# Twenty-two halves of the shared expert units moved beside the first group's score maxima

## What is computed

```python
xn = layernorm(x)                                    # x: (4, 1024, 256)
q, k, v = xn @ Wq + bq, xn @ Wk + bk, xn @ Wv + bv   # 16 heads of 16
attn = softmax(where(causal, q @ k.T / sqrt(16), -inf)) @ v
scores = softmax(xn @ gate_w.T)                      # (4096, 16)
w, idx = top_k(scores, 4);  w = w / sum(w)
routed = sum_e combine[:, e] * ((silu(xn @ w_gate[e]) * (xn @ w_up[e])) @ w_down[e])
shared = (silu(xn @ sw_gate) * (xn @ sw_up)) @ sw_down
out = x + (attn @ Wo + bo) + routed + shared
```

## Time and profile before

| | us |
|---|---|
| median of 3 runs | 1351.32 (1346.31 to 1351.62) |
| the profiled execution, in all | 1356.54 |
| its span, first to last instruction | 1354.9 |
| PE busy in the span | 1007.9 |
| DVE busy | 866.0 |
| ACT busy | 654.5 |
| POOL busy | 579.2 |
| mean granted TensorE clock | 0.88 of full |

### The profile page before, as it was taken

The page is one execution under the profiler, slowest core; times in us unless marked ns, Lnnn a source line. Parts: engine busy times, 40 slices in busy tenths (PEclk is TensorE's granted clock), DMA queues, the critical chain, the costliest instruction groups (busy, mean ns, idle before and its releaser), DMA issues.

```text
span 1354.9 us, 26394 instructions
## 1 busy us (share of the span) xinstructions
PE 1007.9 (74%) x8634; PEld 525.7 (39%) x8634; DVE 866.0 (64%) x1784; ACT 654.5 (48%) x1219; POOL 579.2 (43%) x531
## 2 busy tenths in 40 slices
PE   2788121010399999898998989998988989899885
PEld 1555010000144444444544444454444445444433
DVE  6888831000288887777777676676767676677553
ACT  3778100000154545565566666556666665566341
POOL 6333177776200000454366666435656553464100
PEclk9888555555599999899999999999989999899888
DMA  6899450010113131443545355354535353444702
GB/s 175 270 297 283 125 180 1 1 34 1 43 56 105 54 104 48 88 85 75 89 80 112 63 111 95 66 89 78 111 57 112 56 112 64 88 71 73 134 17 31
DMA packets 99484, 126.41 MB, mean 93 GB/s; under 512 B 24873, under 2 KB 83514, under 8 KB 98834
## 3 DMA queue, kind: packets, MB, share of 16 engines
q0 software_dynamic: 41632, 60.79, 25.0%
q1 hardware_dynamic: 57730, 63.99, 16.1%
HBM read 71.63 MB, written 57.80 MB: 96 GB/s over the span
## 4 chain that ended last, share of the span: by engine, by line
PE 53%; DVE 10%; another core or an unknown queue 10%; issue 9%; ACT 2%; SPq 1%; DMA 1%; POOL 0%; ACTq 0%; DVEq 0%
PE gup L1221 12%; PE pvp L1144 10%; PE outs L1248 9%; DVE part L1314 6%; PE smp L1100 6%; PE turn L1233 4%; PE stp L1125 4%; PE outs L1151 3%; PE turn L1191 3%; PE smp L1083 1%; ACT probs L1484 1%; DVE hf L1371 1%; DVE sg L1366 1%; DMA Qs<-nm 1%
## 5 line engine op out<-in xcount | busy, mean ns | idle before, releaser
L1484 ACT ACTIVATE probs<-stp 128x1024 f32<-128x1024 f32 (+1 forms) x320 | 300.4, 939 | 424.4 <-remote 205.2
L1314 DVE TENSOR_REDUCE part<-smp 128x2 f32<-128x256 f32 (+2 forms) x372 | 345.9, 951 | 140.0 <-remote 72.5
L942 POOL DMA_INDIRECT XG<-xrow_d,slots x144 | 146.8, 1019 | 247.0 <-DMA out<-Y 201.7
L1221 PE MATMUL gup<-gu_w,XC 128*128 (+1 forms) x1152 | 212.8, 321 | 32.7 <-issue 21.8
L1100 PE MATMUL smp<-Ks,Qs 48*128 48x128 f16 (+2 forms) x744 | 112.5, 341 | 103.7 <-DVE part L1314 52.4
L1248 PE MATMUL outs<-dn_w,h 88*128 (+1 forms) x1248 | 183.6, 280 | 0.1
L949 POOL DMA_INDIRECT out<-Y,slots x72 | 117.1, 1626 | 139.1 <-ACT Y L1517 107.8
L1144 PE MATMUL pvp<-probs,Vs 128*32 128x512 f32 (+3 forms) x1536 | 168.8, 512 | 0.8 <-DVE probs L1413 0.7
L949 POOL DMA_INDIRECT acc_d<-Y,slots x72 | 114.7, 1594 | 123.7 <-ACT Y L1517 104.6
L1221 PEld LDWEIGHTS gup<-gu_w,XC 128*128 128x128 f16 x1152 | 107.2, 99 | 96.1 <-issue 43.5
L931 POOL DMA_INDIRECT slot_d<-entry,slot_i x128 | 124.3, 971 | 41.6 <-issue 41.6
(11 more groups left out here) (170 smaller groups left out, 1109.6 us busy)
## 6 DMA issues: line engine op xcount, KB each, us to landing
rb<-rsum_d SPq DMA_DIRECT2D x60, 128.0 KB
Ks<-k_d SPq DMA_DIRECT2D x96, 64.0 KB
Qs<-q_d SPq DMA_DIRECT2D x96, 64.0 KB
v_d<-V SPq DMA_DIRECT2D x8, 544.0 KB, 4.6
Vs<-v_d SPq DMA_DIRECT2D x16, 272.0 KB, 3.0
acc_d<-YA SPq DMA_DIRECT2D x1, 4224.0 KB
X<-L_attn_x POOLq DMA_DIRECT2D x8, 512.0 KB, 5.0
xrow_d<-XR SPq DMA_DIRECT2D x8, 512.0 KB, 5.0
```

What stands on the lines that cost most here:

```text
L942: pool.indirect_dma_start(XG[:, q].rearrange("p a c t -> p (a c t)"), None, s.xrow_d, bass.IndirectOffsetOnAxis(ap=slots[:, r, 0:1], axis= ...
L1221: last = pe.matmul(gup[:, 0:2 * I], columns[:, a, h], weights_of(s.gu_w, e, b, h, slice(0, 2 * I)), start=n == 0, stop=n == 5)
L1314: last = dve.tensor_reduce(part[:, g % 2, k0 // CH, :, j, t], banks[:, :, col:col + w], AX.X, ALU.max)
L1484: act.activation(to, of, ACT.Exp, scale=float(DK) ** -0.5 / QS ** 2).then_inc(exp_done, 1)
```

## The change

The planner takes `PRE = 22` halves off the list first and puts them into steps (-1, 0) to (-1, 21), one each; they are firsts of the units 0 to 11 and seconds of 0 to 9. The rest is spread over the slots as before, with a smaller cost per slot; and while the slot is below `READY = 50` the first half of unit 47, the last one before the routed rows, is held back. On PE, DVE and ACT the head becomes a loop of 22 steps: in each of the first 18 a piece of the maxima and then the half of the step, in the last four only the half; `turn_max(0)` comes in step 19 ahead of the half, `close_max(0)` and `send_to_rows(0)` on DVE in step 18. On SP the columns and rows of tiles 0 and 1 come first, then the loads and stores that belong to the halves of steps 0 to 17, then `send_max(0)`, then the two clears, then what belongs to steps 18 to 21.

```diff
+            for m in range(PRE):
+                (first, second)[halves[i][0]][-1, m] = halves[i][1]
+                i += 1
+            per_slot = (sum(cost[i:]) + sum(fixed_work(g, n) for g, n in every)) / (len(every) - SPARE)
             for k, x in enumerate(every):
                 used += fixed_work(*x)
                 for _ in range(2):
+                    if k < READY and i < len(halves) and halves[i] == (0, SU - 1):
+                        continue
...
-        LAG, SPARE = 2, 4
+        LAG, SPARE, PRE, READY = 2, 4, MP + 4, 50
...  (SP)
+            for t in range(2):
+                shared_columns(t)
+                shared_rows(t)
+            for m in range(MP):
+                after_halves(-1, m)
+            send_max(0)
             sp.wait_ge(a_const, 2)
             sp.dma_start(s.acc_d.rearrange("(t p) d -> p t d", p=P),
                          YA[:, 0:1].broadcast_to([P, TT + 1, D])).then_inc(cleared, 16)
             sp.dma_start(s.out[ST * P:T, :], s.xf[ST * P:T, :]).then_inc(cleared, 16)
-            for t in range(2):
-                shared_columns(t)
-                shared_rows(t)
-            send_max(0)
+            for m in range(MP, PRE):
+                after_halves(-1, m)
...  (PE)
-            for m in range(MP):
-                max_piece(0, m, (smp, stp)[m % 2], m - 1)
-            turn_max(0)
-            pe.wait_ge(red_done, MP)
+            for m in range(PRE):
+                if m < MP:
+                    max_piece(0, m, (smp, stp)[m % 2], m - 1)
+                if m == MP + 1:
+                    turn_max(0)
+                if (-1, m) in FIRST:
+                    gate_up(FIRST[-1, m])
+                else:
+                    z = SECOND[-1, m]
+                    turn_h(z)
+                    if z:
+                        down(z - 1, projected)
+                    youts = outs_before(z)
+            pe.wait_ge(red_done, MP)
...  (DVE)
-            for m in range(MP):
-                reduce_piece(0, m, (smp, stp)[m % 2])
-            close_max(0)
-            send_to_rows(0)
+            for m in range(PRE):
+                if m < MP:
+                    reduce_piece(0, m, (smp, stp)[m % 2])
+                if m == MP:
+                    close_max(0)
+                    send_to_rows(0)
+                if (-1, m) in FIRST:
+                    silu_times_up(FIRST[-1, m])
+                else:
+                    low_part(SECOND[-1, m])
+                    after_second(SECOND[-1, m])
...  (ACT)
+            for m in range(PRE):
+                if (-1, m) in FIRST:
+                    gates(FIRST[-1, m])
+                else:
+                    second_half(SECOND[-1, m])
```

## The result

The changed kernel takes 1391.96 us (median of six runs, 1388.21 to 1395.03), the kernel before 1351.47 beside it: 1.0297 times as long, 95% interval 1.0267 to 1.0328. The forecast was 1366, slower by 1.1%. So the sign was right and the size was not: +40 us of median, +36.7 of span, where +15 had been worked out.

A forecast was written before the change was run, and what follows sets the result against it. PE was taken to set the pace outside a stall of late results from POOL's dense indirect DMAs. 26 + 2.5 - 21 + 1.5 + 5 + 1 = +15 us: span 1370, median 1366; range 1318 to 1392 (own 1359 to 1375).

The forecast's parts named there:

- the stall, its cause and its end: POOL's dense indirect DMAs make PE's results late, 2.8 us a matmul; the stall ends at 362 as before.
- Count by 362: Matmuls PE gets through until 362, halves and maxima together: about 125, against 159 in the kernel before.
- two unknowns: In the count by 362: 20 more matmuls, or 12 fewer if scatters take effect some 4 us earlier; neither taken.
- The 13 steps: Head steps of maxima pieces and halves left after 362: 26 us taken, ends 19.5 and 39.
- slots 0 and 1: Their score pieces, done by 362 in the kernel before, now come on top: 2.5 us.
- the row of maxima: From the send of the first maxima to the first score matmul, overlapping steps 20 and 21: +1.5 us.
- The clears: PE waits near slot 2 for columns queued behind the moved clears: +5 us, ends 0 and 12.
- The light slots: Slots 45 to 49 hold no half and are bound by score, exponential and hops: +1 us, ends 0 and 5.
- The halves out of the slots: 20 halves leave the good stage, their PE work nearly all time: -21 us, ends -13 and -23.
- The fourth rival: Poor overlap in the head, steps over 2.8 us, and clears at full cost: +35 us, 1386; chance 0.16.

The follow-up runs named there:

- with 32 rows: Kernel before with the 128 scatters of slot entries carrying 32 rows in place of 128, nothing between them (result incomplete): 1352.61 us, one run.
- both edits: Changed kernel with the two clears sent right after the first four loads and the first routed half not held to slot 50: 1367.46 us, ratio 1.0104.
- The thin kernel: Kernel before with two matmuls in place of six in the gate and up product of 40 routed halves (80 to 119): 1350.30 us, ratio 0.9973.

## Why the prediction was right or wrong

**Right: the stall, its cause and its end.** The stall is in its place with the same 2.8 us a matmul, the halves share it with the maxima and don't fill it, and the scatters make it (156 us, and the graded runs with spaced scatters). The Trainium skill's rule that had been weighed against this (SBUF — State Buffer, Who interferes with whom: TensorE and ScalarE never wait on anyone) does not describe this case, where 103 matmuls are done beside the scatters and 1393 without them; it is a rule on ports, and no run shows what is shared here. The maxima of the first group did run on after 362, to 375.8 and not 385, and the clears did come into fast work. That the end at 362 hangs on POOL's last indirect DMAs, as the forecast took it, is not shown: with 32 rows they were issued 10 us earlier and the stall ended at 362 all the same.

**Count by 362: too low.** 160 matmuls in place of 125. The good time lasted longer than to 178: PE's timeline has 72 matmuls begun by 185 us, where the forecast's working gives about 50, and DVE's last prompt reduction starts at 183.36 (180.76 before). Of the two unknowns named there the favourable one came true; the other, that without the clears the scatters take effect 4 us earlier, did not. By 351.50 ten of 18 pieces were through, and eight were left in place of nine.

**The 13 steps, slots 0 and 1, the row of maxima: 30 forecast, 21 measured.** With the clears early the second close is at 432.97 against 411.69: +21.3, in which these three stand together (the slots up to there hold about as many halves in both kernels; four other kernels with the head of before have that close at 411.1 to 413.2). A step took (375.81 - 362.17)/8 = 1.7 us and not 2.0.

**The clears: 5 forecast, 15 to 19 measured, outside the ends of 0 and 12.** The step that failed is how long the columns take. SP began the clears at 379.53; PE had its columns at 401.27, 22 us later and not 15 to 18, and it wanted them 14.6 us earlier, 7 after the clears began and not 11. The forecast counted the 15 us of full DMA engines and let SP's hold run inside them. SP reached the load of the columns only at 392.00, 12.5 us after it began the clears, and from there it took 9.3 us in place of 2.4. The DMA engines were full only to about 395 (their share is 0.16 from 395 to 397), so why the load took until 401 stays open. From 390.9 to 404.6 PE's clock is at its lower level besides, after PE had stood still from about 387:

```profile
390.90:404.60 13.70, 3.33 (x14) 0.93 (x14) 0.68 (x2) 0.32 (x1) 0.00 (x0) 0.50 1.03 267
```

**The light slots: 1 forecast, 6 to 7 measured, outside the ends of 0 and 5.** The step that failed is that hops alone were priced, and the clock was not: it fell for 13.7 us, in which PE was then busy for 11.0.

**The halves out of the slots: -21 forecast, between -9 and 0 measured.** This is the largest error. From the second close to the last one, before, after, and after with both edits:

```profile
411.69:1262.40 850.71, 778.01 (x6911) 401.74 (x6908) 625.50 (x1148) 503.93 (x932) 381.74 (x290) 0.98 0.43 83
```

```profile
PE smp L1100 <- DVE part L1314: 16.2, 24, 2.3
PE turn L1191 <- issue: 13.8, 23, 2.5
PE gup L1221 <- DVE hf L1371: 9.2, 19, 1.2
```

```profile
447.74:1297.70 849.96, 761.79 (x6769) 391.00 (x6766) 613.56 (x1113) 495.98 (x912) 383.49 (x290) 0.97 0.43 81
```

```profile
PE smp L1113 <- DVE part L1337: 24.2, 29, 3.2
PE turn L1204 <- issue: 20.5, 29, 3.2
PE gup L1234 <- DVE hf L1394: 13.3, 23, 1.6
```

```profile
433.28:1275.70 842.42, 756.46 (x6770) 388.30 (x6767) 612.61 (x1113) 496.79 (x912) 384.35 (x290) 0.98 0.43 82
```

```profile
PE turn L1204 <- issue: 22.2, 30, 4.0
PE smp L1113 <- DVE part L1337: 19.0, 23, 3.3
PE gup L1234 <- DVE hf L1394: 14.8, 22, 1.6
```

PE is busy 16 us less and the stretch is 0.7 us shorter; with the light slots gone (the last two fences) it is 21.6 of PE's and 8.3 of time, still outside the forecast's ends of -13 and -23. What is missing stands in PE's waits. In that last kernel they are 22.2 in place of 13.8 ahead of the turning of routed rows, 14.8 in place of 9.2 for DVE's products of the unit before, and 19.0 in place of 16.2 for DVE's reductions. "PE is 95% busy, so nearly all of it is time" is the step that failed. The 95% was read in one stage of 58 us, and over the whole stretch PE was busy 778.0 of 850.7, 91%; and a busy share, either one, doesn't say what taking work out brings. The thin kernel shows it apart from the change: 18 us less of busy PE, 3 us of time. No single wait carries what is missing, and which chain sets the lower bound of a slot stays open, since no run shortened one.

**The sum again, with measured terms:** 21.3 (head) + 14.8 (clears) - 0.7 (second close to last close: light slots about +7.5, halves -8.3) + 1.4 (after the last close, 92.5 before and 93.9 after) = 36.8; the span grew by 36.7. The terms I gave had errors of -9, +10, +6 and +13: three of four on the same side, each time because work on a quiet path was taken to be hidden or work on the busy engine to be time. The fourth rival (1386, 39 for the steps and 12 for the clears) came nearer in its number, and half of its mechanism was there: the clears cost more than its 12, but the poor overlap in the head did not occur (1.7 us a step where it needed over 2.8). That 1391.96 still lies inside the stated 1318 to 1392, at its very edge, is luck: no case there had the halves bring so little.

## What to carry to other kernels

A busy share above 90% says what work added to that engine costs; what taking work away brings must be asked separately, and a run that thins one engine's work and nothing else tells it: here 22.7 us more of it cost 20 and 18 us less brought 3, partly because the clock fell. Before work is moved into a stall, find what makes the stall: here the filler shared it, while a filling of 0.54 us between the instructions that caused it took 9% off the kernel. A bulk transfer that is moved out of a stall delays whatever is loaded behind it, here by 12.5 us until the load was issued and 9.3 more until it could be used. A row of light slots can cost the clock as well.

## What the runs showed of the hardware

Indirect DMAs that GpSimd issues 1.2 to 1.3 us apart, 128 in a row, hold back TensorE's results to one matmul in 2.8 us, whether they carry 128 rows or 32 of 8 bytes. At 1.41 us apart 287 matmuls got through in 183 us, at 1.51 982, at 1.62 1341, from 1.73 on about 1390, the number without any. Why is open: the traces show matmuls begun promptly once they are released and their completions seen late, and nothing of what lies between. Open too is when the stall ends. In all nine traces with the scatters not spaced out its end lies between 359.6 and 363.0 us, both where the last scatter was issued at 336 and the last gather at 349, and where they were issued at 322 and 339.
